# Moving the transpose of the score maxima behind the four-group run of value products in a fused DiT block

## The reference

```python
h = layernorm(x) * (1 + scale_msa) + shift_msa
q, k, v = split(h @ Wqkv + bqkv)                  # 16 heads of 32
attn = softmax(q @ k.T * 32 ** -0.5)              # 1024 x 1024 for each head
x = x + gate_msa * ((attn @ v) @ Wproj + bproj)
h = layernorm(x) * (1 + scale_mlp) + shift_mlp
x = x + gate_mlp * (gelu(h @ W1 + b1) @ W2 + b2)  # 512 -> 2048 -> 512
out = rmsnorm(x) * (1 + emb_scale) + emb_shift
```

## Time and profile before

| | us |
|---|---|
| median of 3 runs | 4009.19 |
| lowest and highest | 4009.13, 4010.85 |
| the profiled execution, its own time | 4011.15 |
| its span, first to last instruction | 4009.4 |
| TensorE busy in the span | 3947.7 (98%) |
| VectorE busy | 2414.3 (60%) |
| ScalarE busy | 1812.7 (45%) |
| GpSimd busy | 1927.4 (48%) |

### The profile page before, as it was taken

How to read it: one execution, slowest core, us unless ns; L and a number is a source line. 1 busy time by engine, 2 the same in 40 slices (tenths; PEclk the granted TensorE clock), 3 DMA queues, 4 the chain that set the end, 5 groups by cost and what they waited for, 6 DMA issues and landing times.

```text
span 4009.4 us, 51892 instructions
## 1 busy us (share of the span) xinstructions
PE 3947.7 (98%) x19723; PEld 2717.3 (68%) x19723; DVE 2414.3 (60%) x4020; ACT 1812.7 (45%) x3220; POOL 1927.4 (48%) x562
## 2 busy tenths in 40 slices
PE   8999999999999999999999999999999999999998
PEld 6777886445555555555555554788888888888886
DVE  3665557787878878787887875333443433344442
ACT  2222223666666666666666666333333333333332
POOL 1000004788888888887888888632112222221221
PEclk9999999999999999999999999999999999999999
DMA  5444463333233233323323332411011112111110
GB/s 197 180 180 163 185 218 94 75 70 77 59 88 75 65 76 78 79 59 88 75 65 77 78 80 64 124 35 43 35 43 35 48 40 66 43 35 43 35 43 21
DMA packets 184996, 323.72 MB, mean 81 GB/s; under 512 B 14452, under 2 KB 53428, under 8 KB 184748
## 3 DMA queue, kind: packets, MB, share of 16 engines
q1 hardware_dynamic: 184748, 320.41, 28.0%
HBM read 201.77 MB, written 117.54 MB: 80 GB/s over the span
## 4 chain that ended last, share of the span: by engine, by line
PE 93%; DVE 3%; DMA 2%; issue 1%; ACT 1%; POOL 0%; SPq 0%; POOLq 0%; ACTq 0%; DVEq 0%
PE psum L997 12%; PE psum L535 12%; PE psum L1008 12%; PE psum L436 10%; PE psum L437 10%; PE psum L438 10%; PE psum L1519 6%; PE psum L1515 6%; PE psum L1517 6%; PE psum L1024 5%; PE psum L1038 4%; DVE max_part L825 2%; PE psum L1477 1%; PE psum L471 1%; PE psum L543 0%
## 5 line engine op out<-in xcount | busy, mean ns | idle before, releaser
L825 DVE TENSOR_REDUCE max_part<-psum 128x1 f32<-128x512 f32 x2048 | 1288.6, 682 | 299.2 <-PE psum L535 292.7
L1118 ACT ACTIVATE probs<-psum 128x512 f32<-128x512 f32 x2048 | 1095.0, 599 | 619.3 <-PE psum L997 609.5
L1226 POOL TENSOR_TENSOR prob_sum<-prob_sum,probs 128x2048 f32<-128x2048 f32 x256 | 1176.8, 4597 | 29.5 <-ACT probs L1118 0.9
L535 PE MATMUL psum<-k_stack,q_stack 96*128 96x512 f32 x2048 | 771.5, 407 | 3.7 <-DVE max_part L825 1.7
L1648 DVE TENSOR_TENSOR g_parts<-g_full,g_parts 128x512 fp32r<-128x512 f32 x256 | 263.2, 1028 | 818.3 <-ACT g_parts L1557 818.3
L997 PE MATMUL psum<-q_stack,k_stack 98*128 98x512 f32 x2048 | 741.2, 408 | 4.9 <-issue 3.8
L997 PEld LDWEIGHTS psum<-q_stack,k_stack 98*128 98x128 f32 x2048 | 383.2, 190 | 247.6 <-issue 109.8
L1553 ACT ACTIVATE g_full<-psum,cols 128x512 f32<-128x512 f32 x256 | 176.6, 690 | 815.7 <-PE psum L438 815.4
L1715 POOL TENSOR_TENSOR y_out<-y_out,rows 128x512 f32<-128x512 f32 x64 | 82.9, 1296 | 936.4 <-DVE y_out L1686 936.4
L535 PEld LDWEIGHTS psum<-k_stack,q_stack 96*128 96x128 f32 x2048 | 383.3, 190 | 208.4 <-DVE max_part L825 122.8
L1008 PE MATMUL psum<-probs,v_group 128*32 128x512 f32 x4096 | 503.6, 598 | 0.0
(11 more groups left out here) (152 smaller groups left out, 4759.9 us busy)
## 6 DMA issues: line engine op xcount, KB each, us to landing
qk_parts<-qk_out SPq DMA_DIRECT2D x128, 512.0 KB, 2.8
k_stack<-qk_parts SPq DMA_DIRECT2D x96, 512.0 KB, 7.1
q_stack<-qk_parts SPq DMA_DIRECT2D x192, 256.0 KB, 9.4
x_in<-in_x SPq DMA_DIRECT2D x16, 1024.0 KB, 5.4
v_rows<-v_out SPq DMA_DIRECT2D x64, 256.0 KB, 2.0
v_group<-v_rows SPq DMA_DIRECT2D x32, 512.0 KB, 4.0
gated_attention<-gated SPq DMA_DIRECT2D x64, 256.0 KB, 4.6
x<-in_x SPq DMA_DIRECT2D x16, 1024.0 KB, 8.2
```

Source lines behind the costliest of these rows:

```text
L535: pe.matmul(psum[:, SMAX[at.turn % 3], :], q_stack[u % 3][0:PARTS, h, i * P:(i + 1) * P], k_stack[G % 2][0:PARTS, h, kh * CH:(kh + 1) * CH ...
L825: dve.reduce_max(max_part[:, n:n + 1], psum[:, SMAX[at.turn % 3], :], AX.X).then_inc(dve_smax, 1)
L1118: act.activation(probs[slot(u, kt)][:, h, :], psum[:, ST[n % 3], :], ACT.Exp, scale=SCALE).then_inc(act_exp, 1)
L1226: pool.tensor_tensor(total[:, :, :], total[:, :, :], probs[slot(u, kt)][:, :, :], ALU.add).then_inc(pool_sum, 1)
```

## The change

In ORDER the mark `!` moves from ahead of `nV` to behind it. On TensorE the transpose T of the maxima stands behind the fourth V of the run instead of behind the third. On VectorE the step `n` now stands ahead of the reading of the transposed maxima. On SyncE no letter of its own lies between the two places, except a V that triggers nothing there (only the second V of a unit does), so its list of DMAs keeps its order. The number of m ahead of the mark stays 16, so LEAD (line 53) and with it the run-ahead of the maxima are unchanged.

```diff
-    ORDER = ("sgmsmsmsmDsmsmmssmasVDmssmsmmswDVtmrmmspssmVVV!n"
-             "VssmjmjmjjsjmsmssmjmjsmsjmjssmsmjsjmsmmjsssmmVV")
+    ORDER = ("sgmsmsmsmDsmsmmssmasVDmssmsmmswDVtmrmmspssmVVVnV"
+             "!ssmjmjmjjsjmsmssmjmjsmsjmjssmsmjsjmsmmjsssmmVV")
```

## The result

The changed kernel takes 3989.24 us (median of 4 runs, 3987.79 to 3990.75), the kernel before beside it 4010.02 us (4009.13 to 4011.03). The ratio is 0.9945, with a 95% interval from 0.9933 to 0.9957: 20.8 us or 0.52% faster. The forecast was 3995.3 us, in a range from 3992 to 4003. The direction was right, the gain was half as large again as forecast, and the time lies 2.8 us under the range.

What follows compares the result with a forecast made beforehand. TensorE's own stream was taken as the bound. Behind the run, 0.86 + 0.13 + 0.31 + 0.24 = 1.54 us replaced 1.78; 62 units x 0.23 less 0.4 gave 13.9 us, so 3995.3 us, range 3992 to 4003.

Steps and rivals of the forecast that it cites:

- T to the next matmul, 0.13 us: TensorE behind the run: the score after T was to start 0.13 us behind T's start.
- the row at 631 us: Timeline row of a T among full-width matmuls, after a TensorE wait; source of the spacings 0.13 and 0.31 us.
- 0.33 for the score behind T: Chain from end to end: the first score behind T was to take 0.33 us, in a sum of 1.64.
- rival C: The score's weight load is wholly hidden behind T: gain 0.31 us a unit, 19.2 us, to 3990; chance 0.06.
- unit 63: At its start TensorE waits for the sent maxima; no 0.23 us gain there, and 0.4 us charged for later sending.
- the cover by n: On VectorE, n (0.67 us) fills the idle 0.93 us of waiting for T and ends before T; no cost.
- D: Slower: TensorE waits at the third m for VectorE's reading of T's bank; 26.3 us more, 4035; chance 0.03.
- the third m: It writes T's bank after VectorE's readings; 0.71 us to spare, 0.24 in the 9 units without projection products.
- A: T counts as a form of its own, its border costing like a run's: gain 7.7 us, 4001.5; chance 0.12.
- B: Nothing changes: the 0.23 us return as a longer start of the scores; 4009.2, up to 4010; chance 0.07.

Runs made afterwards that it cites:

- e4: Changed kernel with one of the two scores behind the run put between the third and fourth V; 4012.0 us, ratio 1.0001 to the kernel before.
- e8: Changed kernel with one run fewer per unit, the first D beside the first V and the second D; 3999.6 us, ratio 0.9970 to the kernel before.
- e9: As e8, but scores and maxima spread evenly around that run; 3989.2 us, ratio 0.9941 to the kernel before.
- e10: As e9, but eight scores ahead of the run, five behind it and two maxima side by side there; 3995.4 us, ratio 0.9955 to the kernel before.
- e12: As e9, with one pair of scores side by side ahead of the last two maxima of each stretch; 3989.2 us, ratio 0.9944 to the kernel before.
- e1: Kernel before with only n moved ahead of the reading of the maxima, T left behind the third V; 4011.1 us, ratio 1.0001.
- e3: Changed kernel with T two scores later, among full-width matmuls; 4000.8 us, ratio 0.9973 to the kernel before.
- e2: Kernel before with only T moved behind the fourth V, n left behind the reading of the maxima; 4040.6 us, ratio 1.0068.
- e11: The changed kernel itself, measured again; 3990.6 us, ratio 0.9943 to the kernel before.

## Why the prediction was right or wrong

**Right: the bound and the frame.** TensorE's own stream was the thing to cost, T does cut the run in two, a V inside a run costs 0.86 and the run of four 3.57. e4 confirms the border as the cause, e8, e9, e10 and e12 put the same 0.33 us on a run taken away, and e1 shows that n moved alone gives nothing.

**Wrong: the term "T to the next matmul, 0.13 us", from the row at 631 us**. In a stream it is 0.03 (changed kernel, e3, e4). The row at 631 us was the wrong neighbour for the reason that the prediction named and then let pass: TensorE had waited there. e9, e12 and e2 show what a wait does in this kernel: the weights of the waiting matmul are loaded only when it starts, and the matmul behind it comes 0.10 us later than it would. The 0.13 at 631 us fits that as 0.03 and 0.10: T's weights are loaded there at 631.07, 0.03 ahead of T, where in e3 it is 0.23. That isn't the whole of it, since behind a run T's load also starts only with T (1519.96) and the score still follows after 0.03. Nothing was run at that place itself, so why that row is 0.10 us longer than the rows of a stream stays open. With 0.03 the sum reads 0.86 + 0.03 + 0.31 + 0.24 = 1.44, and 1.78 - 1.44 = 0.34, which is what a unit with products lost (29.23 to 28.89). The end-to-end sum has the same fault in "0.33 for the score behind T"; it was 0.23.

**Wrong with it: the range.** Its lower end came from leaving rival C out at 0.06. C's time, 3990, was the right one. Its mechanism was half right: the row that I asked for, a matmul spaced 0.24 behind the one that follows T, isn't there from start to start (it is 0.31 to 0.33), but in the chain the score behind T costs a plain 0.23. A row taken behind a wait should have bounded the cost from one side only.

**Right in the sum, with a wrong size: unit 63.** T's later sending was charged with 0.4 us. The score can start 1.85 us behind the start of the run of two V ahead of it; by that TensorE's wait grew from 0.19 us (2478.32 against 2478.13) to 0.38 (2454.74 against 2454.36), so 0.2 was lost. That is one execution each, and the DMA itself took 8.16 us in one and 7.69 in the other.

**Right but too briefly told: the cover by n.** "Its price is nothing" held in the changed kernel. What it costs if that cover is gone was not worked out; e2 shows 0.85 us a unit, more than twice the gain. This is the step on which the sign of the change hangs, and the prediction spent its slower rival (D) on the third m instead. Of that margin, in the units without products, 0.24 us had been reckoned. The trace after shows next to none: the three m there take 0.88 us and not 0.85, the score behind them starts 0.02 late, and TensorE's loads waited for line 844 nine times, 1.6 us in all.

**The rivals.** A (T as a form of its own, 4001.5) and B (nothing changes) are refuted by the result, whose interval ends at 0.9957, and again by e11. D didn't occur in the changed kernel; its wait, the third m for line 844, is what costs the nine units of e3 their 0.36 us.

## What to carry to other kernels

On an engine that is full, count the changes between narrow and full-width matmuls: each run of narrow ones costs a fixed third of a microsecond here, and a short full-width step belongs behind a run, not in it. When a step is moved on one engine, look at what its partner on another engine now stands behind: the same move was worth 21 us with n ahead and minus 29 without. Take the price of an operation from a row in a running stream, for here every row behind a wait carried 0.1 us that belong to the wait or its place.

## What the hardware showed unexpectedly

- The border of a run has three parts: 0.10 us on the way in (0.33 instead of 0.23 from the last m to the first V), 0.13 at the run's end and 0.10 at the first full-width matmul behind. The Trainium skill (TensorEngine Tiling (Array Packing), Key Properties) says that a change of mode drains the array. The traces agree that the change costs and put 0.33 us on the pair of changes (e4); the drain itself isn't seen in them.
- One T of 16 columns behind a run costs 0.02 us, each further one 0.11, one among full-width matmuls 0.12.
- A wait of a matmul costs 0.1 us more than its length: 0.03 us of waiting moved the stream by 0.13 (e9), 0.75 by 0.85 (e2). So a stream that is barely outrun loses far more than the wait list shows; in e9 and e12 that took back nearly all that the missing run was worth.
